# Feed-forward phase of a decoder layer: the square of the hidden layer and its low part change engines

## The reference

```
h   = x2 @ (w * scale).T + gate * (x2 @ v.T @ fast_b.T @ u.T)   # 256 -> 1024, one weight here: wfc
r   = maximum(h, 0)
y   = (r * r) @ (ternary weight).T * pscale                     # 1024 -> 256
out = layernorm(x2 + y)
```

## Time and profile before

| what | us |
|---|---|
| median of three runs | 1457.17 |
| the profiled execution, its own time | 1455.03 |
| its span in the trace | 1453.2 |
| PE busy in the span | 1362.2 (94%) |
| DVE busy | 910.7 (63%) |
| ACT busy | 835.9 (58%) |
| POOL busy | 631.3 (43%) |
| all h_lo of POOL, 64 instructions | 89.4 |
| all rr of ACT, 64 instructions | 39.4 |

### The profile page before, as it was taken

One profiled execution on the slowest core, in us unless ns is written; L12 is line 12 of the kernel. 1 busy time (PEld: TensorE's weight loads), 2 busy tenths in 40 slices (PEclk: granted clock), 3 DMA queues, 4 the chain that ended last, 5 costly groups with the idle time before them and its releaser, 6 DMA issues. The chain is left out here.

```text
span 1453.2 us, 20706 instructions
## 1 busy us (share of the span) xinstructions
PE 1362.2 (94%) x7068; PEld 881.7 (61%) x7068; DVE 910.7 (63%) x1755; ACT 835.9 (58%) x1126; POOL 631.3 (43%) x312
## 2 busy tenths in 40 slices
PE   6999768999999999999999999999999997699996
PEld 5767545556566655656665665666566563477664
DVE  5678736674765666476566646656664664376765
ACT  2334435664656566465656646565665654668774
POOL 3512004563544455354545535454553544345443
PEclk8999979999999999999999999999999999799998
DMA  5211120000100100010010001001000100001101
GB/s 178 91 58 58 59 90 1 1 1 1 60 1 1 60 0 0 0 60 0 0 60 0 0 0 60 0 0 60 0 0 0 44 1 15 29 31 43 58 15 43
DMA packets 25532, 42.83 MB, mean 29 GB/s; under 512 B 3440, under 2 KB 7936, under 8 KB 25488
## 3 DMA queue, kind: packets, MB, share of 16 engines
q1 hardware_dynamic: 24672, 39.10, 7.9%
q0 software_dynamic: 816, 3.15, 0.7%
HBM read 29.66 MB, written 12.58 MB: 29 GB/s over the span
## 5 line engine op out<-in xcount | busy, mean ns | idle before, releaser
L905 DVE CUSTOM_DVE_ANT_0 junk<-ps,mask 128x512 bf16<-128x512 f32 x512 | 319.9, 686 | 102.0 <-PE ps L1029 100.6
L727 POOL TENSOR_TENSOR acc<-prob 128x1024 f32<-128x1024 f32 x64 | 153.2, 2394 | 501.0 <-ACT prob L771 501.0
L771 ACT ACTIVATE prob<-ps,mcol 128x1024 f32<-128x1024 f32 x256 | 281.5, 1117 | 135.2 <-PE ps L1023 129.3
L730 POOL TENSOR_TENSOR acc<-acc,prob 128x1024 f32<-128x1024 f32 x128 | 303.9, 2374 | 11.5
L1044 PE MATMUL ps<-prob,v_b 128*64 128x512 f32 x1024 | 245.0, 599 | 0.0
L1044 PEld LDWEIGHTS ps<-prob,v_b 128*64 128x64 f32 x1024 | 69.2, 136 | 131.5 <-issue 107.6
L1240 POOL TENSOR_TENSOR h_lo<-relu,h_hi 128x512 fp32r<-128x512 f32 x64 | 89.4, 1405 | 106.7 <-ACT relu L1283 106.7
L1021 PE MATMUL ps<-q_hi,k_hi 64*128 64x512 f32 x512 | 115.3, 445 | 3.1 <-ACT shift L798 1.6
L910 DVE TENSOR_TENSOR ps<-ps,recip 128x512 f32<-128x512 f32 x64 | 44.8, 699 | 116.3 <-ACT recip L786 116.1
L1029 PE MATMUL ps<-k_hi,q_hi 64*128 64x512 f32 x512 | 102.1, 393 | 2.7 <-DVE nmx L905 2.0
L1023 PE MATMUL ps<-shift,ones_r 64*128 64x512 f32 x512 | 101.8, 391 | 0.0
(11 more groups left out here) (204 smaller groups left out, 2901.0 us busy)
## 6 DMA issues: line engine op xcount, KB each, us to landing
x_in<-in_xT SPq DMA_DIRECT2D x8, 512.0 KB, 3.7
x_scratch<-x_a SPq DMA_DIRECT2D x8, 512.0 KB, 2.8
raw<-x_scratch SPq DMA_DIRECT2D x8, 512.0 KB, 5.1
raw<-in_cT SPq DMA_DIRECT2D x8, 512.0 KB, 5.9
x_res<-x_scratch SPq DMA_DIRECT2D x8, 512.0 KB, 4.5
y_scratch<-y SPq DMA_DIRECT2D x8, 512.0 KB, 3.2
y_c<-y_scratch SPq DMA_DIRECT2D x8, 512.0 KB, 3.7
outT<-x SPq DMA_DIRECT2D x8, 512.0 KB, 2.8
```

Of the source, the lines that this page charges most:

```text
L727: pool.tensor_tensor(total, prob[:, 0], prob[:, 1], ALU.add).then_inc(acc_out, 1)
L730: pool.tensor_tensor(total, total, prob[:, kt], ALU.add).then_inc(acc_out, 1)
L771: act.activation(prob[:, i].rearrange("p h t -> p (h t)"), SCORE[i % 2].rearrange("p h t -> p (h t)"), ACT.Exp, scale=SCALE, bias=mcol[:, ...
L905: dve.tensor_tensor_reduce(junk[:, t % 2, h], SMAX[t % 2][:, h], mask[:], -1.0, -LOWEST, ALU.add, ALU.min, nmx[:, t, h * DH:h * DH + 1]).t ...
```

## The change

`rr` moves from ACT to POOL: POOL now multiplies r by itself. It waits for the relu of the tile and, from the fifth tile on, for the `h_lo` of four tiles before, which frees the buffer of rr. `h_lo` moves from POOL to DVE as `hidden_lo`. ACT loses its third instruction of each tile; its relu now waits for the product of four tiles before, which frees the buffer of r. The first batch of POOL stands outside its loop.

```diff
-                    pool.wait_ge(hi_out, HK * b + i + 1)
-                    pool.wait_ge(rr_out, HK * b + i + 1)
-                    pool.tensor_tensor(h_lo[:, i, :], rr[:, i % RH, :], f32(h_hi[:, i, :]),
-                                       ALU.subtract).then_inc(lo_out, 1)
+                    pool.wait_ge(relu_out, HK * b + i + 1)
+                    if not (first and i < RH):
+                        pool.wait_ge(lo_out, HK * b + i - RH + 1)
+                    n = i % RH
+                    pool.tensor_tensor(rr[:, n, :], r[:, n, :], r[:, n, :], ALU.mult).then_inc(rr_out, 1)
...
+                if not (first and i < RH):
+                    act.wait_ge(rr_out, n - RH + 1)
                 act.activation(r[:, i % RH, :], HIDDEN[i % RH], ACT.Relu).then_inc(relu_out, 1)
...
                 act.activation(h_hi[:, i, :], r[:, i % RH, :], ACT.Square).then_inc(hi_out, 1)
-                if not (first and i < RH):
-                    act.wait_ge(lo_out, n - RH + 1)
-                act.activation(rr[:, i % RH, :], r[:, i % RH, :], ACT.Square).then_inc(rr_out, 1)
...
+            def hidden_lo(b, i):
+                n = HK * b + i
+                dve.wait_ge(hi_out, n + 1)
+                dve.wait_ge(rr_out, n + 1)
+                dve.tensor_tensor(h_lo[:, i, :], rr[:, i % RH, :], f32(h_hi[:, i, :]), ALU.subtract).then_inc(lo_out, 1)
...
                     sum_y3(b - 1, second)
+                hidden_lo(b, 0)
+                hidden_lo(b, 1)
                 if not last:
                     deviate2(b + 1, False)
+                hidden_lo(b, 2)
                 if not last:
                     sum_squares2(b + 1, False)
+                hidden_lo(b, 3)
                 if not first:
                     deviate3(b - 1, second)
+                for i in (4, 5):
+                    hidden_lo(b, i)
                 if not first:
                     sum_squares3(b - 1, second)
+                for i in (6, 7):
+                    hidden_lo(b, i)
                 if not last:
                     normalise2(b + 1, 1 - par, False)
```

More of the change, by code:

```diff
@@ L1234, in _, with batch @@
             pool.tensor_copy(tern[:], c["tern"][:]).then_inc(tern_out, 1)
-            def batch(b):
+            def batch(b, first):
                 for i in range(HK):
-                    pool.wait_ge(hi_out, HK * b + i + 1)
-                    pool.wait_ge(rr_out, HK * b + i + 1)
-                    pool.tensor_tensor(h_lo[:, i, :], rr[:, i % RH, :], f32(h_hi[:, i, :]),
-                                       ALU.subtract).then_inc(lo_out, 1)
-            with pool.Fori(0, B) as b:
-                batch(b)
+                    pool.wait_ge(relu_out, HK * b + i + 1)
[3 more added lines that the diff above has]
+                    pool.tensor_tensor(rr[:, n, :], r[:, n, :], r[:, n, :], ALU.mult).then_inc(rr_out, 1)
+            batch(0, True)
+            with pool.Fori(1, B) as b:
+                batch(b, False)
         @block.scalar
```

## The result

The changed kernel takes 1465.45 us (median of 7 runs, 1464.03 to 1467.11), the kernel before 1456.65 in the same comparison: a ratio of 1.0059 (95% interval 1.0044 to 1.0075). It is slower, as forecast, but by 9 us where 22 were forecast. The time lies just inside the lower edge of the range given (1464 to 1487) and under the main case's own (1470 to 1484), so the size of the effect was forecast more than twice too large. The profiled executions say the same: span 1462.5 us against 1453.2, 9.3 more.

What follows compares the result with a forecast made beforehand. PE was taken as close to the limit, standing 1.13 us per batch for cx_lo, which ACT made late. Terms -0.2 + 1.3 + 18 + 3.1 = +22 us on 1455.03 gave 1477.2, stated as 1478; range 1464 to 1487.

Steps and rivals of the forecast that it cites:

- main case: DVE's queue becomes the limit of a feed-forward batch, 3.6 us longer; 1478 us, own range 1470 to 1484, chance 75%.
- the price of the square: POOL's product of r with itself takes 1.30 us as h_lo did, and holds the pair for 1.16.
- First interval: No earlier batch's work on DVE, mostly held by PE's lower starting clock: saved ACT time less blocked h_lo, -0.2 us.
- Second: The second interval lacks normalise3, 2.3 us on DVE: 3.6 - 2.3 = +1.3 us.
- The five others: Five more intervals between ends of cx_lo, each 3.6 us longer since DVE's queue is the limit: +18 us.
- The last batch: h_lo 0 to 3 and POOL's squares go in steps of 1.7 us, so var3 and all behind it move +3.1 us.
- the lock-out: DVE's instruction with two SBUF inputs and POOL's never run together: one waits, then needs 0.54 (1.08 if 1024 wide) or 1.16 us.
- Full hiding: With a square of about 0.9 us, PE's wait of 1.3 us becomes about 0.3: -7, 1448 us; chance 7%.
- Good packing: POOL's squares fall beside DVE's PSUM instructions, no idle time on DVE, a batch of 24.2 us: +6, 1461 us; chance 9%.
- Lower clock: PE's waits grow to 2 to 3 us and its clock drops ahead of var3: 1478 + 12 = 1490 us; chance 9%.

Runs made afterwards that it cites:

- costs: The kernel before with 21 two-input POOL instructions added behind its last batch: 1.262 us for two different tiles, 1.038 for one tile named twice.
- two_tensors: The changed kernel, but POOL multiplies r by a constant weight tile instead of by itself: 1479.54 us, ratio 1.0145 to the kernel before.
- rr_act: The kernel before with only h_lo moved to DVE; rr stays on ACT and POOL has no instruction in the batches: 1460.53 us, ratio 1.0023.
- dev2_first: The changed kernel with deviate2 ahead of the first two h_lo on DVE instead of behind them: 1459.47 us, ratio 1.0015 to the kernel before.
- mix_pool: The kernel before with only the squares rr of tiles 2 and 7 moved to POOL: 1453.13 us against 1455.97, ratio 0.9981.

## Why the prediction was wrong in size

**The step that failed** is the price of the square: "I take 1.30, of which 1.16 hold the pair, since the instruction still names two inputs." It measured 1.04, 0.90 on the pair, because both inputs name one tile (costs). The prediction saw this case and gave it 7%, but priced it only at its far end, a square of 0.72, from the nearest one-input row; the truth lay between the two rows. The rule of the Trainium skill, "GPSIMD Engine Reference", section "2.1 Instruction dispatch", that both operands go one after the other through one read port, pointed to the length of `h_lo` and so to the same mistake; it fits the 1.262 us of two different tiles, and for one tile named twice the measurement, 1.038, decides against it. The lock of the Trainium skill's "SBUF — State Buffer", section "SBUF: two separate sides", agrees with the rows here, with one refinement: the part that has to wait for the other engine is 0.13 to 0.15 us shorter than the whole instruction (0.54 of 0.69 us, 1.08 of 1.21, 0.90 of 1.04, 1.16 of 1.30). The sum is steep in this price: with 1.26 us (two_tensors) the phase was 22.5 us longer than before (25.9 in span less the 3.4 ahead of it), 22.2 were forecast for 1.30; with 1.04 it is 9.1. That 22.5 and 22.2 agree so well is in part luck: with the long square the five later intervals grew by 16.5 where 18 were forecast and the first fell by 1.0 instead of 0.2, and the last batch, 5.4 for 3.1, made up for both.

**Term by term**, from the ends of `cx_lo`:

- First interval: -0.2 forecast, -2.25 measured (22.97 against 25.22). With the long square it is -1.0, so some 1.2 of the 2.05 missed is the square's price. The rest is a misreading: ACT's third instruction did cost the first batch time (rr_act, which has it, takes 25.22 there, dev2_first, which has not, 22.68), and PE's low clock was not what held it (0.91 over this interval in the kernel before and 0.91 in the changed one).
- Second: +1.3 forecast, +0.1 measured; with the long square +1.6.
- The five others: +18 forecast, +8.6 measured (24.29, 25.22, 25.25, 25.23, 25.03 against 23.3 or 23.1); with the long square +16.5. This is the bulk of the error.
- The last batch: +3.1 forecast, +2.75 measured, but this is luck. The forecast moves var3, and with it all behind it, by 3.1 (`h_lo` and square in steps of 1.7); var3 moved by 1.7 only, from 14.7 us behind `cx_lo` to 16.4. Another 1.0 is PE's lower clock, which the sum had left out: ahead of the last mean PE stood 2.36 us instead of 1.58, and the matmul pair took 2.08 instead of 1.12.

The two rows of the changed kernel's last batch:

```profile
1438.99 1.12 PE L1469 MATMUL ps<-sq_sum,mean_w 128*128 128x512 f32 x2 [1.52 <-DVE sq_sum L1318]
1447.04 2.08 PE L1465 MATMUL ps<-y_sum,mean_w 128*128 128x512 f32 x2 [2.36 <-DVE y_sum L1318]
```

**What held.** The direction and the lock-out, with `h_lo` at 1.05 with POOL and 0.69 without. ACT waits for `deviate2` with relu 3 queued behind, PE waits for var2 and var3, and DVE has no idle time ahead of `rs`, as forecast; all of it is in the rows above. The four kernels with rr and the place of deviate2 changed apart split the loss of a loop batch: neither cause 23.3, deviate2 late alone 24.1, lock-outs alone 23.7, both 25.2. Together they cost more (1.9) than the sum of the two (0.8 + 0.4), which reads as a late relu 3 that packs the last five squares and DVE's last instructions into one stretch (POOL has five of its eight squares from 1332.58 on in the batch above); no run tests this by itself. dev2_first also has rr off ACT, so its 0.4 is what lock-outs cost less what the relief of ACT gives.

**The rivals.** "Full hiding" was right in its premise that a tile named twice costs less, wrong in its size. "Good packing" forecast 1461 for another reason: it had no idle time on DVE, and the batch shows 1.6 us of it. "Lower clock" did not occur in the loop of the changed kernel (1.00) but did in its last batch, and in part with the long square.

## What to carry to other kernels

When the sum rests on an instruction of which the trace has no row, work the sum out at both ends and in the middle of its price before giving a range: here 0.22 us of length, 64 times, on a half-idle engine were some 13 us of time, through a shared resource that two queues take in turns. Work moved to an engine with idle time is not free where its list has a step that another engine waits for: put what others wait for (here `deviate2`) ahead of what only has to be done by the end. And move as much as clears the wait that was seen, not all of it: at most 1.3 us per batch were to be had, and two squares of eight were enough to remove PE's wait for `cx_lo` (mix_pool, 0.7 us of a batch), four squares and three `h_lo` brought 0.2 more, where the whole change cost 9 us.

## What the runs showed of the hardware

- A POOL instruction with two float32 inputs of 128x512 takes 1.262 us alone for two different tiles, two buffers of one tensor included, and 1.038 for one tile named twice. On DVE no such difference is seen: the square of one 1024-wide tile takes 1.21, as `cx_lo` with two different ones does (1.23).
- The pair is taken in turns to the hundredth: in the changed kernel a square that starts during DVE's `x` ends 0.90 us behind it, and an `h_lo` behind a square ends 0.54 or 0.55 us behind it (1335.31 against 1334.77). `x` is a scalar_tensor_tensor with two SBUF inputs, so this form locks POOL out as well; in the phase before the change none of them met a POOL instruction.
- PE's clock: a two-part statistics matmul took 1.12 us behind waits of 1.1 to 1.6 us, and 2.08 behind 2.36 in the last batch of the changed kernel; but 2.08 also behind 0.95 and 1.12 close together in two_tensors, and behind waits of 2.2 us in that kernel both occur: 2.07 twice, 1.12 to 1.16 four times. The length of the last wait alone does not tell which level it gets.
